# Moving the sums of weight blocks between products, and the start of attention for batches 4 and 5, in a fused attention and feed-forward kernel

## The reference

```python
x = x + xattn(layernorm(x), ctx)     # h = gelu_tanh(x1) * x1 with x1 = xn @ ctx.T;  h @ ctx; 120 context rows
n = layernorm(x)
h = silu(n @ W1.T * s1) * (n @ W2.T * s2)        # 256 -> 1024
h = gelu(h @ H1.T * t1)                          # 1024 -> 1024, exact gelu
h = gelu(h @ H2.T * t2)                          # 1024 -> 1024
x = x + h @ W3.T * s3                            # 1024 -> 256
```

## Time and profile before

| | us |
|---|---|
| median of 3 runs (lowest, highest) | 376.11 (374.9, 377.42) |
| the profiled execution, its own time | 377.62 |
| its span in the trace | 375.8 |
| PE busy in the span | 336.9 (90%) |
| DVE busy | 276.2 (73%) |
| ACT busy | 218.9 (58%) |

### The profile page before, as it was taken

How to read it: one execution, slowest core, us unless ns; L and a number is a source line. 1 busy time by engine, 2 the same in 40 slices (tenths; PEclk the granted TensorE clock), 3 DMA queues, 4 the chain that set the end, 5 groups by cost and what they waited for, 6 DMA issues and landing times.

```text
span 375.8 us, 4801 instructions
## 1 busy us (share of the span) xinstructions
PE 336.9 (90%) x1636; PEld 278.8 (74%) x1636; DVE 276.2 (73%) x508; ACT 218.9 (58%) x367; POOL 31.5 (8%) x62
## 2 busy tenths in 40 slices
PE   7799997999904999999997999999994699999995
PEld 5689885788802788888995888887782488888894
DVE  4587989589954387987578559589787547787884
ACT  2448373383704374587923566867776456578770
POOL 6140102000000000310002002000000000000000
PEclk9999999699965799999999999999998599999999
DMA  6899566766978266345310533653584245576003
GB/s 162 257 336 383 198 225 260 301 225 189 367 302 297 91 213 233 112 131 205 113 58 0 170 112 112 222 180 104 175 267 130 102 166 178 167 235 206 0 2 118
DMA packets 24557, 68.61 MB, mean 183 GB/s; under 512 B 1744, under 2 KB 3152, under 8 KB 21968
## 3 DMA queue, kind: packets, MB, share of 16 engines
q1 hardware_dynamic: 17328, 51.47, 39.6%
q0 software_dynamic: 7200, 16.78, 14.6%
HBM read 57.75 MB, written 10.49 MB: 182 GB/s over the span
## 4 chain that ended last, share of the span: by engine, by line
PE 64%; DVE 14%; ACT 8%; issue 7%; DMA 5%; POOL 0%; DVEq 0%; ACTq 0%; POOLq 0%
PE P L1304 39%; PE P L1255 13%; PE P L1333 7%; ACT TR L618 4%; DMA blocks_h<-SLY 2%; DVE H L909 2%; DMA SLY<-in_h 2%; DVE H L930 2%; PE P L1208 2%; PE P L1219 1%; ACT H L634 1%; PE P L1227 1%; DVE TR L920 1%; DVE H L887 1%; ACT SLY L608 1%
## 5 line engine op out<-in xcount | busy, mean ns | idle before, releaser
L1304 PE MATMUL P<-TR,WR 128*128 128x512 f32 x896 | 216.0, 402 | 23.1 <-DVE H L930 22.1
L1304 PEld LDWEIGHTS P<-TR,WR 128*128 128x128 f32 x896 | 171.9, 194 | 64.8 <-issue 14.8
L914 DVE TENSOR_TENSOR TR<-H,TR 128x512 fp32r<-128x512 f32 x112 | 76.1, 687 | 41.8 <-ACT TR L618 40.0
L618 ACT ACTIVATE TR<-H 128x512 fp32r<-128x512 f32 x112 | 69.0, 626 | 26.9 <-DVE H L909 26.6
L1255 PE MATMUL P<-X,W 128*128 128x512 f32 (+1 forms) x320 | 65.6, 362 | 1.6 <-DVE X L876 1.6
L1255 PEld LDWEIGHTS P<-X,W 128*128 128x128 f32 x320 | 53.5, 195 | 10.6 <-DVE X L876 2.0
L656 ACT ACTIVATE H<-H,sc 128x512 f32<-128x512 f32 x40 | 28.9, 721 | 33.9 <-DVE H L930 33.9
L887 DVE SCALAR_TENSOR_TENSOR H<-P,sc,SLY 128x512 f32<-128x512 f32 (+1 forms) x40 | 25.4, 639 | 24.5 <-PE P L1255 19.7
L909 DVE TENSOR_TENSOR H<-H 128x512 f32<-128x512 f32 x64 | 41.9, 684 | 0.0
L634 ACT ACTIVATE H<-P 128x512 f32<-128x512 f32 x48 | 27.8, 594 | 20.9 <-PE P L1304 20.9
L608 ACT ACTIVATE SLY<-P,sc 128x512 f32<-128x512 f32 (+1 forms) x40 | 23.1, 598 | 20.5 <-PE P L1255 20.3
(11 more groups left out here) (72 smaller groups left out, 211.0 us busy)
## 6 DMA issues: line engine op xcount, KB each, us to landing
WR<-blocks_h SPq DMA_DIRECT2D x16, 1024.0 KB, 5.7
WR<-in_h POOLq DMA_DIRECT2D x12, 1024.0 KB, 6.2
H<-in_h SPq DMA_DIRECT2D x6, 1024.0 KB, 12.8
blocks_h<-H SPq DMA_DIRECT2D x6, 1024.0 KB, 5.1
xn<-in_h SPq DMA_DIRECT2D x8, 512.0 KB, 3.7
xt<-in_h SPq DMA_DIRECT2D x8, 512.0 KB, 3.7
W<-in_w POOLq DMA_DIRECT2D x4, 512.0 KB, 6.2
SLY<-in_h SPq DMA_DIRECT2D x2, 1024.0 KB, 6.2
```

Of the source, the lines that this page charges most:

```text
L618: eng.activation(TR[:, f % RING, 0, :], operand(c, L, s, kk), ACT.Copy).then_inc(s_hi, 1)
L914: eng.tensor_tensor(TR[:, f % RING, 1, :], operand(c, L, s, kk), TR[:, f % RING, 0, :].bitcast(f32), ALU.subtract).then_inc(s_lo, 1)
L1304: out_ = eng.matmul(bank(c, L, s, m)[:, :], WR[r % WRING][:, at:at + 128], TR[:, f % RING, h, :], start=(s in FRESH[L] and kk == 0 and h = ...
```

## The change

Five things are moved. (1) Raw eighths 4 and 5 are loaded by POOL into the two halves of X, each when `layer1` has done with it, and summed there; q=6 goes to SLY, q=7 to the quarter of H1 that q=5 had. So no eighth waits for another's buffer. (2) The sums stand elsewhere in DVE's list: `combine(3)` moves from step m=0 of `layer1(1)` to m=5, `combine(4)` to m=7 of it, `combine(5)` behind the differences for product 2, `combine(6)` behind those for product 6, `combine(7)` behind those for product 4; none is left between the totals. (3) In both chunks `total(c,0,(1,1),.)` is four operations in a row, followed by four `lo`, instead of taking turns; ACT likewise does the four `hi` first; chunk 1's tests 14 and 15 stand behind them. (4) In `layer1(1)` and `layer1(3)` the differences for product 1 are taken at m=0 to 3 and their low parts at m=2 to 5. (5) Batches 4 and 5 do all of their attention inside the last layer of chunk 0, with batches 6 and 7 one step later than before: `stats(0,4)`, `scale(0,4)` and those of 5 take the place of those of 6 and 7 in `square(0)`. Besides, PE takes the banks of product 0 of layer 1 in the order 2, 3, 0, 1 in its first step. The pieces of the diff below belong, in this order, to the places in memory, SP, POOL, DVE (`layer1`, `late_products`, the last layer) and PE.

```diff
-        AREA = {0: (0, 0, 1), 1: (0, 1, 1), 2: (1, 1, 1), 3: (1, 0, 1), 5: (1, 1, 0), 7: (0, 1, 0)}
+        AREA = {0: (0, 0, 1), 1: (0, 1, 1), 2: (1, 1, 1), 3: (1, 0, 1), 7: (1, 1, 0)}
         def raw(q):
-            if q in (4, 6):
+            if q in (4, 5):
+                return X[:, q - 4, :, :, :].rearrange("p h k t -> p (h k) t")
+            if q == 6:
                 return SLY[:, :, :]
...
-            load_raw(4)
-            load_raw(5)
-            load_sum(0, 0, 4)
+            load_raw(6)
             sums_out(4)
             load_raw(7)
-            load_raw(6)
+            load_sum(0, 0, 4)
             sums_out(5)
...
-            rstds(4, (0, 3), (1, 2), (1, 3), (0, 4), (0, 5))
+            rstds(4, (0, 3), (1, 2), (1, 3))
+            for q in (4, 5):
+                eng.wait_ge(s_mm1, 16 * (q - 2))
+                eng.dma_start(raw(q), h2[:, q - 4, :, :]).then_inc(s_raw[q], 16)
...
-                    if t == 1:
-                        if m == 0:
-                            combine(3)
-                        if m in (1, 2):
-                            stats(0, 3 + m)
-                        if m in (3, 4):
-                            scale(0, 1 + m)
-                    if t % 2 == 1 and m % 2 == 0:
-                        add(t // 2, 0, 1, m // 2)
-                    if m in (3, 5, 7):
-                        lo(t // 2, 0, t % 2, m // 2 - 1)
+                    if t == 2 and m < 2:
+                        scale(0, 6 + m)
+                    if t % 2 == 1 and m < 4:
+                        add(t // 2, 0, 1, m)
+                    if t % 2 == 1 and 2 <= m <= 5:
+                        lo(t // 2, 0, 1, m - 2)
+                    if t == 1 and m in (5, 7):
+                        combine(3 + m // 6)
...
                 for i in range(4):
                     total(c, 0, (0, 1), i)
                     lo(c, 0, 6, i)
-                if c == 0:
-                    combine(6)
-                    combine(7)
-                else:
-                    test(BESIDE[1, 0, 4])
                 for i in range(4):
                     total(c, 0, (1, 1), i)
+                for i in range(4):
                     lo(c, 1, 0, i)
                 if c == 1:
+                    test(BESIDE[1, 0, 4])
                     test(BESIDE[1, 0, 6])
...
-                    if c == 0 and k in (0, 1):
-                        last(c, 1, k)
+                    if c == 0 and k in (1, 3):
+                        resid(4 + k // 2)
                     if c == 0 and k in (4, 5):
-                        resid(k)
-                    if c == 0 and k in (6, 7):
-                        scale(1, k - 2)
+                        scale(1, k)
                 if c == 0:
                     second(4)
                     second(5)
+                    last(c, 1, 0)
+                    last(c, 1, 1)
...
-                if (t, i) == (1, 10):
-                    turn(0, 4)
-                    turn(0, 5)
-                if t == 2 and i in (3, 5):
-                    turn(0, 5 + i // 2)
+                if t == 2 and i in (5, 7):
+                    turn(0, 4 + i // 2)
...
             def attend4(half, k):
                 if (half, k) == (1, 1):
+                    turn(0, 4)
+                    turn(0, 5)
+                if (half, k) == (1, 3):
                     score(4)
                     score(5)
-                if (half, k) == (0, 0):
+                if (half, k) == (1, 7):
                     weigh(4)
                     weigh(5)
-                if (half, k) == (0, 7):
+                if (half, k) == (0, 6):
                     turn(1, 4)
                     turn(1, 5)
```

More of the change, by code:

```diff
@@ L343, in sums_out @@
                 dst = wS[("h1", "h2")[layer_of(q)]][:, :, q % 4, :].rearrange("s p o -> p s o")
-                eng.dma_start(dst, raw(q)).then_inc(s_S[q], 16)
+                eng.dma_start(dst, raw(q).bitcast(f32) if q in (4, 5) else raw(q)).then_inc(s_S[q], 16)
             def load_sum(c, L, s):
@@ L580, in first @@
                     eng.wait_ge(s_mm1, 16 * t)
+                    raw_left(eng, 2 + t)
                 eng.activation(X[:, t % 2, 0, :, (b % 2) * TB:(b % 2 + 1) * TB],
@@ L692, in late_products @@
                     gelu(c, 0, (0, 1), i)
-                    if i == 2 and (c, 0, 4) in BESIDE:
-                        magnitude(BESIDE[c, 0, 4])
+                for i in range(4):
+                    hi(c, 1, 0, i)
                 for i in range(4):
                     gelu(c, 0, (1, 1), i)
-                    hi(c, 1, 0, i)
-                    if i == 2 and (c, 0, 6) in BESIDE:
-                        magnitude(BESIDE[c, 0, 6])
+                if c == 1:
+                    magnitude(BESIDE[1, 0, 4])
+                    magnitude(BESIDE[1, 0, 6])
             def square(c):
@@ L733, in layer1 @@
                         copy_t(3)
-                    if t == 1 and m >= 6:
-                        copy_t(m - 2)
-                    if t == 2 and m in (2, 3):
-                        copy_t(4 + m)
-                    if m % 2 == 1:
-                        hi(t // 2, 0, t % 2, m // 2)
+                    if t == 2 and m in (3, 4):
+                        copy_t(3 + m)
+                    if t % 2 == 0 and m % 2 == 1:
+                        hi(t // 2, 0, 0, m // 2)
+                    if t % 2 == 1 and 1 <= m <= 4:
+                        hi(t // 2, 0, 1, m - 1)
                     if (t, m) in BESIDE1:
@@ L761, in _ @@
                     hi4(c, 1, 4 + i)
-                    gelu(c, 1, (1, 0), i)
+                    if c == 1 or i < 2:
+                        gelu(c, 1, (1, 0), i)
                 if c == 0:
+                    copy_t(4)
+                    copy_t(5)
+                    gelu(0, 1, (1, 0), 2)
+                    gelu(0, 1, (1, 0), 3)
                     act_s(4)
@@ L972, in square @@
                     if c == 0 and s == 2:
+                        stats(0, 4)
+                        stats(0, 5)
+                    if c == 0 and s == 3:
+                        scale(0, 4)
+                        scale(0, 5)
+                    if c == 0 and s == 6:
                         stats(0, 6)
                         stats(0, 7)
-                    if c == 0 and s == 3:
-                        scale(0, 6)
-                        scale(0, 7)
             def late_products(c):
                 add_up(c, 0, 2)
-                if c == 1:
+                if c == 0:
+                    combine(5)
+                else:
                     test(BESIDE[1, 0, 1])
@@ L988, in late_products @@
                 if c == 0:
-                    combine(4)
+                    combine(6)
                 else:
@@ L993, in late_products @@
                 if c == 0:
-                    combine(5)
+                    combine(7)
                 else:
@@ L1037, in combine @@
             def combine(q):
[L1039 removed]
+                to = raw(q)
+                r = to.bitcast(f32) if q in (4, 5) else to
                 eng.wait_ge(s_raw[q], 16)
[L1041 to L1042 removed]
+                eng.tensor_tensor(to[:, 3, :], r[:, 2, :], r[:, 3, :], ALU.add).then_inc(s_comb, 1)
+                eng.tensor_tensor(to[:, 2, :], r[:, 0, :], r[:, 2, :], ALU.subtract).then_inc(s_comb, 1)
                 eng.wait_ge(s_comb, 4 * q + 1)
[L1044 removed]
+                eng.tensor_tensor(to[:, 0, :], r[:, 3, :], r[:, 0, :], ALU.subtract).then_inc(s_comb, 1)
                 eng.wait_ge(s_comb, 4 * q + 3)
[L1046 removed]
+                eng.tensor_tensor(to[:, 1, :], r[:, 1, :], r[:, 0, :], ALU.subtract).then_inc(s_comb, 1)
             def last(c, half, q):
@@ L1204, in turn @@
                     eng.wait_ge(s_X1, b - 1)
+                if norm == 0 and b in (4, 5):
+                    gelu_done(eng, 0, 1, b, 0)
                 for j in range(2):
@@ L1298, in product @@
                     eng.wait_ge(s_lo, f + 1)
-                    for m in range(4):
+                    for m in (2, 3, 0, 1) if (L, s, kk) == (0, 1, 0) else range(4):
                         if kk == 0:
```

40 lines of the change are left out of this document (14 added, 26 removed).

## The result

The changed kernel takes **358.57 us** (median of 4 runs, 358.08 to 359.3), against 376.0 for the kernel before on the same chip: a ratio of **0.9536** (95% interval 0.95 to 0.9572), 17.4 us less. The forecast was 353.4, its range 347.5 to 360. One later run fell into a slow state: of the six runs with the scores early, one took 555.48 us at a mean granted clock of 0.557, and the figures given there leave it out.

A forecast was written before the change was run, and what follows sets the result against it. PE was taken as the bound, its deep holes mostly waits for `total` followed by low clock. Terms -10.9 (chunk 0), -11.5 (chunk 1) and -0.3 (part 5) sum to -22.7 us: 353.4 us from median 376.11, 8-in-10 range 347.5 to 360.

The forecast's parts named there:

- Part 1, the totals, chunk 0: Product 6 of chunk 0: totals in one piece end nearly all of an 18.6 us loss; PE waits about 0.5 us.
- Counting back from the continuous piece: Before product 6: full-speed product time subtracted from the continuous work's end gives true losses, 18.6 us (chunk 0), 12.3 (chunk 1).
- Part 1, chunk 1: Product 6 of chunk 1: totals ahead of last `lo` and test start it at 285.5, not 297.0: -11.5 us.
- part 4: Earlier differences and low parts in `layer1` remove chunk 1's 0.83 us wait in product 1; counted inside chunk 1's -11.5 us.
- The row that I leaned on: Granted clock in chunk 0's hole: still 1.00 two us after PE fell idle, 0.50 some three us after.
- part 5: Last layer and `layer1(2)`: attention of batches 4 and 5 moved there, net -0.3 us, bounds -2 and +2.
- Part 2, the late sum: Before product 1, chunk 0: later `combine(3)` delays weights, product 1 starts at 79.0 (76.4 to 81.5); chunk 0 net -10.9 us.
- part 3: New memory places and DMA queues: no cost expected; chunk 1's `load_sum(1,1,1)` keeps 2 us of cover.
- the slow side of the forecast: Chunk 0, product 3: raw 5 landing after about 119 makes the kernel slower than before; chance 2%.
- traffic: Before product 1: write 9.3 and load 6.9 us start it at 83.5, total 358 or 361; chance 13%.

## Why the prediction was right, and where it was off

**Part 1, the totals, chunk 0: right.** Forecast: PE waits 0.5 us ahead of product 6, 29 operations in 18.4 us; measured 0.41 and 18.6. Counting back from the continuous piece (18.6 us lost before) was the step that let a hole of 9.9 us with its satellites be priced with its clock.

**Part 1, chunk 1: the wait right, its price not.** I foresaw one wait of 1 to 2 us and reasoned that it was shorter than the idle after which the clock fell. The wait was 1.69 us, but the clock fell after it in this execution and took 1.6 us; -11.5 was forecast for the chunk with part 4, and -10.0 came. The same wait, 1.65 to 1.70 us, went unpunished in four experiments (58.64 to 58.67 us for the 256 matmuls, with raw 5 held back, scores early, and part 5 undone in both versions) and was punished again in the one with the late sum undone (60.14). The row that I leaned on shows when the clock fell in one long hole, not that a short one is safe.

**Part 2, the late sum: mechanism right, size off by one term.** The hole, its releaser and its place were as forecast. Its end was 81.42 instead of 79.0, just inside the bounds given. The step that failed reads "between 4.2 (alone) and 9.3 (two beside it) I take the middle, 6.8, for one beside it": it measured 8.6, which is 1.8 of the 2.4 us. The middle had no row behind it, and the step did not ask which of the two is issued first: raw 5 was, by 0.4 us, and the write paid nearly as much as with two beside it; issued 1.1 us ahead, with part 5 undone, it took 4.4. The other 0.6 us is the sum itself, whose write went out at 67.9 and not at 67.3: 67.9 + 8.6 + 4.9 = 81.4. The load's 4.9 held (4.8). In the other direction low clock cost 1.3 us (30.65 for 128 matmuls against 29.35) where 2.7 was charged, so chunk 0 ended 1.1 us worse, not 2.4. That is luck, since with the scores early the same hole cost 2.7. The 2.7 was loose in itself: half of 5.8 us is 2.9, and the row it came from gives 2.4 (59.69 us for 250 matmuls of 0.229).

The Trainium skill (DMA: Bandwidth & Descriptors, Anatomy of one DMA) states its fit for DMAs that GpSimd issues; for a megabyte it comes to an estimate of 4.4 us. SP's write alone (4.2) and its load (4.7 to 4.9) agree; 8.6 and 7.3 us of SP, and 8.0 of POOL, issued into another DMA of the same size, do not. By that rule without neighbours product 1 would have started at 76.1; the run with raw 5 held back started it at 76.75.

**Part 5: right for the last layer, its side effect not seen.** -0.2 against -0.3. But the move pushed the scores of 6 and 7 back by a step, and with them the load of a test piece that waits for all scores. That cost 1.8 us in products 0 and 5 of chunk 1. I had followed each moved instruction on PE, ACT and DVE, and not asked which DMA counts the moved scores before it is issued.

**Part 4 and part 3: right.** The stretch with the wait of 0.83 us became 0.9 us shorter, and neither SP's queue nor the areas in X made a wait. Raw 7 landed at about 96 us (issued at 79.15, 16.8 us to landing), not before 90 as forecast, but its sum came only at 103.9. The load of raw 5 landed in 6.7 us while DVE worked without pause on sums; so the slow side of the forecast had no ground. The Trainium skill's rule on DVE's shared ports (SBUF — State Buffer, SBUF: two separate sides), named there as a way to a late raw 5, was neither confirmed nor refuted. Raw 5 was loaded with no `scale` near it. Raw 4's load was issued at 47.36, beside a `scale` of 0.82 us at 47.54, and landed in 6.8 us, like raw 5; with so short an operation that decides nothing.

Of the 4.4 us between -22.7 and -18.2 (rounded), chunk 0 is 1.1, products 0 and 5 are 1.8, and the dip at 278 is 1.4 to 1.6. Of the rivals, traffic (358 to 361) has the right total for partly the right reason, a slow write; its product 1 at 83.5 did not come. That the late sum is the large item is shown from both sides: alone it makes the old kernel 2% slower (1.4 to 2.5%), undone it makes the changed one 2.6% faster (0.9286 / 0.9536 = 0.974).

Left open: why a wait of 1.6 to 1.7 us is sometimes followed by half clock and sometimes not, in the same place of nearly the same program. No run separates it. No run has part 1 of chunk 0, or part 4, by itself either; their shares are read from the trace of the changed kernel.

## What to carry to other kernels

When a list on a busy engine is thinned by moving items earlier or later, follow what each item's result or buffer releases: a write and a reload of weights (14 us here), or a load that an engine has in the middle of its queue (2 us at products 0 and 5; 2.25 us ahead of a `gelu`). A gain in front of a hole is worth nothing until the hole is gone; the same part 5 brought little with the weights late (358.57 us with it, 359.64 without, intervals that overlap) and 3.5 us once they were in time. A transfer on the critical path is priced by what is already in flight when it is issued. The average of its price alone and in a crowd came in none of the three runs that show it (SP's transfers took 4.4 and 4.7, or 7.3 and 8.6): ask which one is issued first.
